# First attention of a two-layer block: score matmuls on 64 of the 128 contraction rows, two at a time

## The chip, the cores and the metric

One core of one Trainium2 chip runs the whole program. The metric is device microseconds of one execution, from the first instruction to the end. TensorE's engine is PE in the profile, its weight loader PEld; VectorE is DVE, ScalarE is ACT, GpSimd is POOL, SyncE is SP.

## The reference, cut to what matters

Two layers follow each other on `x` (2 batches of 1,024 tokens, width 256). The first is attention of the tokens over 154 context rows, with 16 heads of width 16:

```python
q = (xq @ Wq + bq).reshape(B, Lq, nh, dh)          # nh = 16, dh = 16
kv = (xkv @ Wkv + bkv).reshape(B, Lkv, 2, nh, dh)  # Lkv = 154
scores = jnp.einsum('bqhd,bkhd->bhqk', q, k) / jnp.sqrt(jnp.float32(dh))
attn = jax.nn.softmax(scores, axis=-1)
out = jnp.einsum('bhqk,bkhd->bqhd', attn, v).reshape(B, Lq, H)
return x_q + (out @ Wp + bp)
```

The second layer (a one-head attention over the same context, a router over 3 experts and a gate) follows it and is not touched by the change. Only the `scores` line above is.

## The kernel before, in words

The first attention works on 16 groups g (`GR`): 4 chunks c of 512 tokens times 4 sets gi of four heads. The 128 partitions of a group hold its four heads with 32 rows each: 16 rows of q rounded to fp32r beside the keys, and 16 rows with the same q beside the low part of the keys. So one head's scores need only 32 of the 128 rows, and the keys `ka` and `kb` are laid out block-diagonally: the columns of head k are zero on all rows but its own 32.

A group passes through these steps on PE, and the name of each is a function in the text below:

- `proj`: q of the group, six matmuls of 128x512 into bank 0 or 1; ACT rounds it to `qh` (L648).
- `rows(g, q)`, q = 0..3: token-major scores of 128 tokens, two matmuls of 308 columns (L1203), one for heads 0 and 1 into one bank of `pair`, one for heads 2 and 3 into the other. They serve only for the maxima: DVE reduces both banks at once (L894). There is one `pair`, so the next `rows` waits for the reduce (`mx_d`).
- `shift`: four small matmuls (L1211) subtract the maxima from q in its bank, and DVE makes `ql`, the low part with the shift (L903).
- `keys(g, k)`: key-major scores of head k's first 128 keys, two matmuls of 512 columns (`ka` with `qh`, `kb` with `ql`, both recorded under the helper's L1110) into bank 2 or 3. The fifth, k = 4, holds the 26 last keys of all four heads. ACT takes the exponential from the bank (L657), and a `keys` waits for the exponential that frees its bank.
- `av`: values times exponentials. Four heads write 32 partitions each, side by side (L1242), then the tails with a full 128x128 matmul (L1245).
- `uz`, `ztr`, `wproj` of the chunk before: transposes (L1255), division on DVE (L910, L913), transposes (L1266), a copy on ACT (L672), the output projection (`wp`, `zt`).

While group g makes its exponentials, group n = g + 1 makes its maxima: the generator `l0_steps` writes the order out by hand, and every engine walks through the same list. `fill[0]` to `fill[5]` are places in it for other work. Of the 16 groups, six (gi 0 and 1 of chunks 1 to 3) have `uz`, `ztr`, `wproj` in `fill[0]`, `fill[1]`, `fill[2]`. Six (gi 0, 1 and 3 of chunk 0, gi 3 of the others) have preparation matmuls for the second layer in `fill[0]` and `fill[2]`, and nothing for PE in `fill[1]`. In the four groups with gi = 2, `fill[0]` and `fill[1]` normalise and transpose the next chunk; in the last chunk they hold front work of the second layer.

Of the kernel before, what the change touches and what calls it, by code (L numbers as in the profile page):

```python
# [31 lines left out]
ACT = mybir.ActivationFunctionType  # L32
AXX = mybir.AxisListType.X

P = 128
B, LQ, D = 2, 1024, 256
LK = 154
NH, DH = 16, 16
# [3 lines left out]
CPB = NC // B  # L42
TJ = CT // P
GH = 4
NG = NH // GH
# [34 lines left out]
def build(nc, dram, out):  # L80
    ctx = ExitStack()
    with ctx:
# [10 lines left out]
        B_S, B_P, B_ST, B_U, B_TOK = [pair[:, i, :] for i in range(2)], bank[0:2], bank[2:4], bank[4], bank[5]  # L93
# [62 lines left out]
        ka, kb = keys_[:, :, :, 0:KAW], keys_[:, :, :, KAW:KAW + KBW]  # L156
# [24 lines left out]
        qh = sb("qh", (P, 2, CT), F32R, l0)  # L181
        ql = sb("ql", (P, 2, CT), F32R, l0)
        z = sb("z", (P, 2, D), F32, l0)
        zt = sb("zt", (P, 2, KC, P), F32, l0)
        pt = sb("pt", (P, GH + 1, CT), F32, l0)
# [55 lines left out]
        k_mm, kh_r, kg_r, v_mm, v_r, ka_r, kb_r = sem("k_mm"), sem("kh_ready"), sem("kg_ready"), sem("v_mm"), sem("v_ready"), sem("ka_ready"), sem("kb_ready")  # L241
# [5 lines left out]
        st_d, ex_d, av_d, u_r = sem("keyscores_done"), sem("exp_done"), sem("av_done"), sem("u_ready")  # L247
# [27 lines left out]
        def l0_steps():  # L275
            yield from (("proj", 0, 0), ("proj", 0, 1))
            for q in range(TJ):
                yield ("rows", 0, q)
                yield ("val", q)
            yield ("shift", 0)  # L280
            yield from (("proj", 1, 0), ("proj", 1, 1))
            yield ("place", 1)
            prep = 0
            for g in range(GR):
                c, gi = divmod(g, NG)
                n, m = g + 1, g + 2


                fill = [()] * 6
                first = list(front1(0))  # L290
                if c > 0 and gi < 2:
                    fill = [(s,) for t in (0, 1) for s in tile_steps(TJ * (c - 1) + 2 * gi + t)]
                if c + 1 < NC:
                    if gi == 0:
                        fill[3] += (("stats", c + 1, 0),)
                        fill[5] += (("stats", c + 1, 1),)
                    elif gi == 1:
                        fill[3] += (("rsqrt", c + 1),)
                        fill[5] += (("norm", c + 1, 0),)
                    elif gi == 2:  # L300
                        fill[0] += (("xt", c + 1, 0), ("norm", c + 1, 1))
                        fill[1] += (("xt", c + 1, 1), ("split", c + 1, 0))
                        fill[2] += (("split", c + 1, 1),)
                for at, place, i in ((GR - 4, 3, 0), (GR - 2, 0, 1), (GR - 2, 5, 2), (GR - 1, 0, 3), (GR - 1, 2, 4),
                                     (GR - 1, 3, 5), (GR - 1, 5, 6)):
                    if g == at:
                        fill[place] += tuple(first[i])

                for i in () if c and gi < 2 else (2, 5) if gi == 2 else (0, 2, 5):
                    if i == (5 if gi == 2 else 2) and c >= CPB:  # L310
                        fill[i] += (("m", 2 * (c - CPB) + gi - 2), ("m_taken", 2 * (c - CPB) + gi - 2))
                    elif prep < len(PREP):
                        fill[i] += (("prep", prep),)
                        prep += 1
                more = n < GR
                order = [("keys", g, 0), more and ("rows", n, 0), ("keys", g, 1), fill[0], ("keys", g, 2),
                         more and ("rows", n, 1), ("keys", g, 3), fill[1], ("keys", g, 4), more and ("rows", n, 2), fill[2]]
                if gi != 2:
                    order += [m < GR and ("proj", m, 0), more and ("rows", n, 3), fill[3], ("av", g), fill[4],
                              more and ("shift", n), m < GR and ("proj", m, 1)]  # L320
                else:

                    order += [more and ("rows", n, 3), fill[3], ("av", g), fill[4], more and ("shift", n),
                              m < GR and ("proj", m, 0), m < GR and ("proj", m, 1)]
                order += [fill[5]]
                for step in order:
                    if step and isinstance(step[0], str):
                        yield step
                    elif step:
                        yield from step  # L330
            assert prep == len(PREP)
# [107 lines left out]
        def walk(steps, parts):  # L439

            for s in steps:
                if s[0] in parts:
                    parts[s[0]](*s[1:])
# [146 lines left out]
        def _(act):  # L590
# [6 lines left out]
            A = nc.scalar.activation  # L597
# [49 lines left out]
                    act.wait_ge(st_d, (GH + 1) * (g - 1))  # L647
                A(qh[:, g % 2, :], B_P[g % 2][:, :], ACT.Identity, bias=sm("bq", g % NG)).then_inc(qh_r, 1)  # L648

            def keys(g, k):  # L650
                n = (GH + 1) * g + k
                act.wait_ge(st_d, n + 1)
                if k == 0 and g:
                    act.wait_ge(av_d, g)
                if n == 0:
                    act.wait_ge(v_r, 2 * B)
                A(pt[:, k, :], B_ST[n % 2][:, :], ACT.Exp, scale=DH ** -0.5).then_inc(ex_d, 1)  # L657

            def av(g):
                c = g // NG  # L660
# [73 lines left out]
                A(th[:, n % TJ, :], gz[:, n % 2, :], ACT.Tanh, scale=0.5).then_inc(th_r, 1)  # L734

            first = {"m_taken": mpiece, "nxf": nxf_, "exp": exp, "wsplit": wsplit, "router": router}
            walk(l0_steps(), {"xt": xt, "proj": proj, "keys": keys, "av": av, "zt": ztr, **first})
            walk(between_steps(), {"zt": ztr, **first})
            walk(l1_steps(), {"nxf": nxf_, "exp": exp, "wsplit": wsplit, "router": router, "hidden": hidden, "gate": gate})

# [359 lines left out]
        def _(pe):  # L1100
            mm = nc.tensor.matmul
# [5 lines left out]
            def passes(dst, terms, first=True, last=True, free=False):  # L1107

                for i, (a, b_) in enumerate(terms):
                    ins = mm(dst, a, b_, start=first and i == 0, stop=last and i == len(terms) - 1,  # L1110
                             skip_group_check=free)
                return ins
# [81 lines left out]
            def rows(g, q):  # L1194
                c, gi = divmod(g, NG)
                n = TJ * g + q
                pe.wait_ge(qh_r, g + 1)
                if gi == 0 and q == 0 and c % CPB == 0:
                    pe.wait_ge(ka_r, c // CPB + 1)
                if n:  # L1200
                    pe.wait_ge(mx_d, n)
                for s in range(2):
                    ins = mm(B_S[s][:, 0:2 * LK], qh[:, g % 2, P * q:P * q + P],  # L1203
                             ka[:, c // CPB, gi, 2 * LK * s:2 * LK * (s + 1)], start=True, stop=True)
                ins.then_inc(s1_d, 1)

            def shift(g):
# [4 lines left out]
                             skip_group_check=True)  # L1212
                ins.then_inc(nm_d, 1)

            def keys(g, k):
                c, gi = divmod(g, NG)
                b = c // CPB
                n = (GH + 1) * g + k
                if k == 0:
                    pe.wait_ge(ql_r, g + 1)  # L1220
                if n == 0:
                    pe.wait_ge(kb_r, 2 * GH)
                    pe.wait_ge(v_r, 2 * B)
                if n >= 2:
                    pe.wait_ge(ex_d, n - 1)
                if k < GH:
                    a, b_ = ka[:, b, gi, LK * k:LK * k + P], kb[:, b, gi, P * k:P * k + P]
                else:
                    a, b_ = ka[:, b, gi, LK * GH:LK * GH + P], kb[:, b, gi, P * GH:P * GH + P]
                passes(B_ST[n % 2][:, :], [(a, qh[:, g % 2, :]), (b_, ql[:, g % 2, :])]).then_inc(st_d, 1)  # L1230

            def av(g):
                c, gi = divmod(g, NG)
                b = c // CPB
                if g == 0:
                    pe.wait_ge(v_r, 2 * B)
                    pe.wait_ge(ones_r, 1)
                else:
                    pe.wait_ge(u_r, g)
                for j in range(GH):  # L1240
                    pe.wait_ge(ex_d, (GH + 1) * g + j + 1)
                    mm(B_U[32 * j:32 * j + 32, :], vmain[:, b, GH * gi + j, :], pt[:, j, :], start=True, stop=False,  # L1242
                       skip_group_check=True)
                pe.wait_ge(ex_d, (GH + 1) * (g + 1))
                mm(B_U[:, :], vtail[:, b, gi, :], pt[:, GH, :], start=False, stop=True,  # L1245
                   skip_group_check=True).then_inc(av_d, 1)
# [154 lines left out]
            def part(c, m):  # L1401
# [7 lines left out]
                for j in range(TJ):  # L1409
                    if r == 0 and q and j % 2 == 0:  # L1410
# [5 lines left out]

            rows_parts = {"uz": uz, "zt": ztr, "wp": wproj, "m": mpiece}
            front_parts = {"nxt": nxt, "score": score, "wtr": wtr}
            walk(l0_steps(), {"xt": xt, "val": val, "proj": proj, "rows": rows, "shift": shift, "keys": keys, "av": av, "prep": prep,
                              **rows_parts, **front_parts})  # L1420
            walk(between_steps(), {**rows_parts, **front_parts})
            walk(l1_steps(), {"nxt": nxt, "score": score, "wtr": wtr, "hidden": hidden, "gate": gate, "part": part})
# [58 lines left out]
```

## Time and profile before

| what | value |
|---|---|
| time, median of 3 runs | 501.45 us (498.39 to 504.14) |
| profiled execution, its span from the first to the last instruction | 497.4 us |
| PE busy | 456.4 us, 92% |
| PEld busy | 357.0 us, 72% |
| DVE, ACT, POOL busy | 326.9, 183.0, 152.1 us |
| granted TensorE clock, mean | 0.986 |
| matmuls of `keys` (L1110, `qh,keys` and `ql,keys`) | 80 and 80 |
| matmuls of `rows` (L1203) | 128 |

The profiled execution has no total time of its own in the record, only its span; the runs' times also hold what lies around the span, and their median is 4.1 us above it.

A busy share of PE counts overlapped matmuls by their modelled ends, so it says that PE was not idle, not that it ran at its peak. What a matmul costs its successor is the distance between two starts: the record of a 128x512 fp32r matmul is 0.40 us long, but the next one starts 0.23 to 0.24 us behind it. In a merged row of the timeline (xN) the length is that of all but the last one's distances plus the last record.

### The profile page before, as it was taken

The page shows a single profiled execution, that of the slowest core. Times are in us where ns is not written, and L with a number is a line of the kernel's source. Part 1 is how long each engine was busy: PE and PEld are TensorE (multiplying, and loading weights), DVE is VectorE, ACT ScalarE, POOL GpSimd, SP SyncE. Part 2 cuts the span into 40 slices and gives each one's busy share as a digit, 9 for nine tenths or more (in the row PEclk, how much of TensorE's full clock was granted, in tenths as well). Part 3 has the DMA queues.
Part 4 walks back from the last instruction along what each step waited for, and adds up shares of the span by engine and source line. Part 5 has one row for each costly group of instructions (what it writes and reads, how often), then busy time and mean ns, then how long its engine had stood idle before and what let it go on. Part 6 is the DMA issues. An engine that isn't in the chain of part 4 may idle for free.

```text
span 497.4 us, 6873 instructions
## 1 busy us (share of the span) xinstructions
PE 456.4 (92%) x2418; PEld 357.0 (72%) x2418; DVE 326.9 (66%) x794; ACT 183.0 (37%) x323; POOL 152.1 (31%) x211
## 2 busy tenths in 40 slices
PE   2657999999999999999977999999999999999994
PEld 2545665776676666766456888888888898888883
DVE  6878757376746754755877448875697657842445
ACT  1260434343344534335442254423444334532210
POOL 9347037204400400100005323354233533315333
PEclk9997999999999999999999899999999999999998
DMA  8701001610020011000011000001000010001001
GB/s 293 310 1 33 10 1 43 234 43 1 21 65 1 1 42 44 0 1 1 1 38 32 0 2 0 2 1 43 1 0 1 3 42 1 1 2 42 1 1 42
DMA packets 7314, 17.45 MB, mean 35 GB/s; under 512 B 880, under 2 KB 2288, under 8 KB 7152
## 3 DMA queue, kind: packets, MB, share of 16 engines
q1 hardware_dynamic: 5040, 11.57, 6.5%
q10 hardware_dynamic: 1584, 3.15, 1.7%
q0 software_dynamic: 656, 2.29, 1.7%
q8 instruction: 20, 0.33, 0.3%
q14 instruction: 14, 0.11, 0.1%
HBM read 14.45 MB, written 2.10 MB: 33 GB/s over the span
## 4 chain that ended last, share of the span: by engine, by line
PE 81%; DVE 11%; issue 3%; POOL 2%; ACT 2%; DMA 1%; POOLq 0%; DVEq 0%
PE bank L1110 52%; PE pair L1110 14%; PE pair L1203 4%; PE bank L1245 3%; PE bank L1242 3%; DVE lnt L783 2%; DVE nm L894 1%; PE bank L1211 1%; PE bank L1255 1%; DVE rs L767 1%; DVE keys L855 1%; DMA ctx_sb<-in_ctx 1%; DVE st L757 1%; PE bank L1266 1%; POOL rs L542 1%
## 5 line engine op out<-in xcount | busy, mean ns | idle before, releaser
L579 POOL TENSOR_TENSOR hs<-hid,hs 128x512 fp32r<-128x512 f32 x48 | 64.2, 1338 | 125.9 <-DVE hs L1063 125.9
L1110 PE MATMUL bank<-nx,w1h 128*128 128x512 f32 x224 | 74.0, 412 | 0.0
L1110 PE MATMUL pair<-w2h,hs 128*128 128x256 f32 x384 | 70.5, 282 | 0.0
L728 ACT ACTIVATE hid<-bank,ab 128x512 f32<-128x512 f32 x48 | 33.0, 689 | 89.6 <-PE bank L1110 89.5
L1110 PEld LDWEIGHTS pair<-w2h,hs 128*128 128x128 f32 x384 | 62.7, 190 | 4.4 <-POOL hs L579 0.2
L894 DVE TENSOR_REDUCE nm<-pair 128x4 fp32r<-128x616 f32 x64 | 51.1, 798 | 19.7 <-PE pair L1203 19.1
L1063 DVE CAST hs<-hid 128x512 fp32r<-128x512 f32 x48 | 20.6, 430 | 57.9 <-ACT hid L728 57.1
L657 ACT ACTIVATE pt<-bank 128x512 f32<-128x512 f32 x80 | 47.2, 598 | 28.6 <-PE bank L1110 26.0
L1110 PE MATMUL pair<-w2l,hs 128*128 128x256 f32 x192 | 54.2, 282 | 0.0
L1110 PE MATMUL bank<-wh,m_ev 128*128 128x512 f32 x112 | 44.5, 398 | 0.0
L1110 PE MATMUL bank<-nx,w1l 128*128 128x512 f32 x112 | 44.4, 396 | 0.0
L541 POOL TENSOR_TENSOR rs<-rs 128x4 f32<-128x4 f32 x21 | 4.5, 215 | 130.2 <-DVE rs L770 129.1
L1110 PEld LDWEIGHTS bank<-nx,w1h 128*128 128x128 f32 x224 | 39.3, 189 | 6.0
L1110 PE MATMUL bank<-qh,keys 128*128 128x512 f32 x80 | 38.2, 477 | 0.2 <-ACT pt L657 0.2
L1110 PEld LDWEIGHTS pair<-w2l,hs 128*128 128x128 f32 x192 | 36.2, 189 | 0.0
L1203 PE MATMUL pair<-keys,qh 128*128 128x308 f32 x128 | 31.8, 330 | 4.0 <-DVE keys L855 3.3
L1203 PEld LDWEIGHTS pair<-keys,qh 128*128 128x128 f32 x128 | 22.4, 191 | 15.3 <-issue 11.7
L666 ACT ACTIVATE u<-bank 128x512 f32<-128x512 f32 x16 | 9.6, 597 | 60.2 <-PE bank L1245 60.2
L1110 PE MATMUL bank<-ql,keys 128*128 128x512 f32 x80 | 31.6, 395 | 0.0
L1080 DVE SCALAR_TENSOR_TENSOR acc<-pair,pr,acc 128x256 f32<-128x256 f32 x48 | 20.1, 476 | 7.6 <-PE pair L1110 7.6
L1110 PEld LDWEIGHTS bank<-wh,m_ev 128*128 128x128 f32 x112 | 21.3, 190 | 5.1
L1110 PEld LDWEIGHTS bank<-nx,w1l 128*128 128x128 f32 x112 | 21.2, 189 | 5.0
(190 smaller groups left out, 921.2 us busy)
## 6 DMA issues: line engine op xcount, KB each, us to landing
stage<-in_w1n POOLq DMA_DIRECT2D x7, 256.0 KB, 3.2
w1e_sb<-in_w1e SPq DMA_DIRECT2D x1, 1792.0 KB, 7.9
x_sb<-in_x SPq DMA_DIRECT2D x3, 512.0 KB, 14.5
stage<-in_w1a SPq DMA_DIRECT2D x3, 512.0 KB, 6.7
stage<-in_ew2T SPq DMA_DIRECT2D x3, 512.0 KB, 3.9
out_x<-x_sb SPq DMA_DIRECT2D x3, 512.0 KB, 2.7
wss_sb<-in_wss SPq DMA_DIRECT2D x2, 512.0 KB, 8.7
x_sb<-in_x ACTq DMA_DIRECT2D x1, 512.0 KB, 4.9
```

The source lines that it names most:

```text
L579: g_.tensor_tensor(hs[:, q % 3, 1, :], hid[:, q % 2, :], hs[:, q % 3, 0, :], ALU.subtract).then_inc(hl_r, 1)
L657: A(pt[:, k, :], B_ST[n % 2][:, :], ACT.Exp, scale=DH ** -0.5).then_inc(ex_d, 1)
L666: A(u[:, g % NU, :], B_U[:, :], ACT.Copy).then_inc(u_r, 1)
L728: A(dst, B_H[n % 2][:, :], ACT.Silu, bias=ab1[:, m, c // CPB:c // CPB + 1]).then_inc(h_r, 1)
L783: return V.tensor_scalar(dst, src, mv[0:rows, t, 0:1], rs[0:rows, 0, t:t + 1], ALU.subtract, ALU.mult)
L894: V.tensor_reduce(nm[:, g % 2, q, :].rearrange("p (h w) -> p h w", w=32)[:, :, DH:DH + 1], pair[:, :, 0:2 * LK].rearrange("p s (a n) -> p ...
L1063: V.tensor_copy(hs[:, q % 3, 0, :], hid[:, q % 2, :]).then_inc(hh_r, 1)
L1080: V.scalar_tensor_tensor(acc[:, j, :], y_tile(j), pr[:, c % 2, j, e:e + 1], acc[:, j, :], ALU.mult, ALU.add).then_inc(y_r, 1)
L1110: ins = mm(dst, a, b_, start=first and i == 0, stop=last and i == len(terms) - 1, skip_group_check=free)
L1203: ins = mm(B_S[s][:, 0:2 * LK], qh[:, g % 2, P * q:P * q + P], ka[:, c // CPB, gi, 2 * LK * s:2 * LK * (s + 1)], start=True, stop=True)
L1242: mm(B_U[32 * j:32 * j + 32, :], vmain[:, b, GH * gi + j, :], pt[:, j, :], start=True, stop=False, skip_group_check=True)
L1245: mm(B_U[:, :], vtail[:, b, gi, :], pt[:, GH, :], start=False, stop=True, skip_group_check=True).then_inc(av_d, 1)
```

## The change

`rows` splits its two matmuls by rows: heads 0 and 1 contract over partitions 0 to 63, heads 2 and 3 over 64 to 127, which leaves out products with zeros only. `keys(g, p)` now takes a pair of heads, p and p + 2, for p = 0, 1: four matmuls of 64 rows, into bank 2 and bank 3, first both `qh` products, then both `ql` products. The tails become a step of their own, `tails(g)`, with all 128 rows, always in bank 2. A pair waits until both banks are free. The list is written anew around it.

```diff
-                order = [("keys", g, 0), more and ("rows", n, 0), ("keys", g, 1), fill[0], ("keys", g, 2),
-                         more and ("rows", n, 1), ("keys", g, 3), fill[1], ("keys", g, 4), more and ("rows", n, 2), fill[2]]
+                order = [("keys", g, 0), more and ("rows", n, 0), fill[0], more and ("rows", n, 1), ("keys", g, 1), fill[1],
+                         more and ("rows", n, 2), ("tails", g), fill[2]]
...
-            def keys(g, k):
-                n = (GH + 1) * g + k
-                act.wait_ge(st_d, n + 1)
...
-                A(pt[:, k, :], B_ST[n % 2][:, :], ACT.Exp, scale=DH ** -0.5).then_inc(ex_d, 1)
+            def keys(g, p):
+                for i in range(2):
+                    n = (GH + 1) * g + 2 * p + i
+                    act.wait_ge(st_d, n + 1)
...
+                    A(pt[:, p + 2 * i, :], B_ST[i][:, :], ACT.Exp, scale=DH ** -0.5).then_inc(ex_d, 1)
+
+            def tails(g):
+                act.wait_ge(st_d, (GH + 1) * (g + 1))
+                A(pt[:, GH, :], B_ST[0][:, :], ACT.Exp, scale=DH ** -0.5).then_inc(ex_d, 1)
...
                 for s in range(2):
-                    ins = mm(B_S[s][:, 0:2 * LK], qh[:, g % 2, P * q:P * q + P],
-                             ka[:, c // CPB, gi, 2 * LK * s:2 * LK * (s + 1)], start=True, stop=True)
+                    r = slice(64 * s, 64 * s + 64)
+                    ins = mm(B_S[s][:, 0:2 * LK], qh[r, g % 2, P * q:P * q + P],
+                             ka[r, c // CPB, gi, 2 * LK * s:2 * LK * (s + 1)], start=True, stop=True)
...
-                if n >= 2:
-                    pe.wait_ge(ex_d, n - 1)
...
-                passes(B_ST[n % 2][:, :], [(a, qh[:, g % 2, :]), (b_, ql[:, g % 2, :])]).then_inc(st_d, 1)
...
+                    pe.wait_ge(ex_d, n)
+                for i in range(2):
+                    r = slice(64 * i, 64 * i + 64)
+                    k = p + 2 * i
+                    mm(B_ST[i][:, :], ka[r, b, gi, LK * k:LK * k + P], qh[r, g % 2, :], start=True, stop=False)
+                for i in range(2):
+                    r = slice(64 * i, 64 * i + 64)
+                    k = p + 2 * i
+                    mm(B_ST[i][:, :], kb[r, b, gi, P * k:P * k + P], ql[r, g % 2, :], start=False, stop=True).then_inc(st_d, 1)
+
+            def tails(g):
...
+                pe.wait_ge(ex_d, (GH + 1) * g + 3)
+                passes(B_ST[0][:, :], [(ka[:, b, gi, LK * GH:LK * GH + P], qh[:, g % 2, :]),
+                                       (kb[:, b, gi, P * GH:P * GH + P], ql[:, g % 2, :])]).then_inc(st_d, 1)
```

`av` takes the heads in the order 0, 2, 1, 3, in which their exponentials now come. DVE's, POOL's and SP's code is the same, and no DMA is moved.

PE's order before, from the start of a group with `uz`, `ztr`, `wproj` up to `wproj` (`keys,qh` into `pair` is `rows`; bank 2 and 3 are `keys`; `ident_sb,u` is `uz`, `ident_sb,z` is `ztr`):

```order
L1110 MATMUL bank3<-qh,keys 128x512
L1110 MATMUL bank3<-ql,keys 128x512
L1203 MATMUL pair<-keys,qh 128x308 x2
L1110 MATMUL bank2<-qh,keys 128x512
L1110 MATMUL bank2<-ql,keys 128x512
L1255 MATMUL bank5<-ident_sb,u 128x128 x4
L1110 MATMUL bank3<-qh,keys 128x512
L1110 MATMUL bank3<-ql,keys 128x512
L1203 MATMUL pair<-keys,qh 128x308 x2
L1110 MATMUL bank2<-qh,keys 128x512
L1110 MATMUL bank2<-ql,keys 128x512
L1266 MATMUL bank5<-ident_sb,z 128x128 x2
```

The same stretch now (L1236 and L1240 are the 64-row matmuls of `keys`, L1209 those of `rows`, L1272 `uz`, L1283 `ztr`):

```order
L1236 MATMUL bank2<-qh,keys 128x512
L1236 MATMUL bank3<-qh,keys 128x512
L1240 MATMUL bank2<-ql,keys 128x512
L1240 MATMUL bank3<-ql,keys 128x512
L1209 MATMUL pair<-keys,qh 128x308 x2
L1272 MATMUL bank5<-ident_sb,u 128x128 x4
L1209 MATMUL pair<-keys,qh 128x308 x2
L1236 MATMUL bank2<-qh,keys 128x512
L1236 MATMUL bank3<-qh,keys 128x512
L1240 MATMUL bank2<-ql,keys 128x512
L1240 MATMUL bank3<-ql,keys 128x512
L1283 MATMUL bank5<-ident_sb,z 128x128 x2
```

Between the first and the second `rows` there were two `keys` and the transposes; only the transposes are left. The third `rows` now follows the second pair and `ztr`, and the tails stand behind it.

In a group with preparation matmuls (`ctxT_sb,pw` here), PE's order from the first `rows` to the tails was:

```order
L1203 MATMUL pair<-keys,qh 128x308 x2
L1110 MATMUL bank2<-qh,keys 128x512
L1110 MATMUL bank2<-ql,keys 128x512
L1110 MATMUL bank5<-ctxT_sb,pw 128x320 x2
L1110 MATMUL bank3<-qh,keys 128x512
L1110 MATMUL bank3<-ql,keys 128x512
L1203 MATMUL pair<-keys,qh 128x308 x2
```

and is now:

```order
L1209 MATMUL pair<-keys,qh 128x308 x2
L1115 MATMUL bank5<-ctxT_sb,pw 128x320 x2
L1209 MATMUL pair<-keys,qh 128x308 x2
L1236 MATMUL bank2<-qh,keys 128x512
L1236 MATMUL bank3<-qh,keys 128x512
L1240 MATMUL bank2<-ql,keys 128x512
L1240 MATMUL bank3<-ql,keys 128x512
L1209 MATMUL pair<-keys,qh 128x308 x2
L1115 MATMUL bank2<-qh,keys 128x512
```

The third `rows` stands directly behind the second pair, with nothing between. Over the whole program, PE's order now has 59 stretches of 64-row matmuls; 50 of them are followed by a 128-row matmul, 9 directly by the 32-column matmuls of `av`.

## Rows read from the trace of the kernel before

**Rows 1.** The page: PE's busy time (us, share, count) and its granted clock in 40 slices.

```profile
PE 456.4 (92%) x2418; PEld 357.0 (72%) x2418; DVE 326.9 (66%) x794; ACT 183.0 (37%) x323; POOL 152.1 (31%) x211
...
PEclk9997999999999999999999899999999999999998
```

**Rows 2.** Busy times by stretch, from the first `keys` to the last `av`.

```profile
49.20:235.80 186.60, 180.72 (x933) 125.37 (x933) 118.09 (x235) 78.34 (x144) 34.70 (x77) 1.00 0.11 34
```

**Rows 3.** The page's groups: busy us, mean ns of one; idle time before, releaser.

```profile
L894 DVE TENSOR_REDUCE nm<-pair 128x4 fp32r<-128x616 f32 x64 | 51.1, 798 | 19.7 <-PE pair L1203 19.1
...
L657 ACT ACTIVATE pt<-bank 128x512 f32<-128x512 f32 x80 | 47.2, 598 | 28.6 <-PE bank L1110 26.0
...
L1110 PE MATMUL bank<-qh,keys 128*128 128x512 f32 x80 | 38.2, 477 | 0.2 <-ACT pt L657 0.2
...
L1203 PE MATMUL pair<-keys,qh 128*128 128x308 f32 x128 | 31.8, 330 | 4.0 <-DVE keys L855 3.3
```

**Rows 4.** Timeline of PE, one undisturbed group with `uz`, `ztr`, `wproj`: start, length.

```profile
205.37 0.50 PE L1110 MATMUL bank<-qh,keys 128*128 128x512 f32 x1
...
205.94 0.45 PE L1203 MATMUL pair<-keys,qh 128*128 128x308 f32 x2
206.22 0.39 PE L1110 MATMUL bank<-qh,keys 128*128 128x512 f32 x1
206.46 0.39 PE L1110 MATMUL bank<-ql,keys 128*128 128x512 f32 x1
206.69 0.60 PE L1255 MATMUL bank<-ident_sb,u 128*128 128x128 f32 x4
...
209.45 1.13 PE L1110 MATMUL bank<-wp_sb,zt 128*128 128x256 f32 x4
210.23 0.58 PE L1110 MATMUL bank<-xh,wqh 128*128 128x512 f32 x1
...
211.40 0.60 PE L1255 MATMUL bank<-ident_sb,u 128*128 128x128 f32 x4
211.93 1.06 PE L1242 MATMUL bank<-pt,vmain 128*32 128x512 f32 x8
212.92 1.12 PE L1245 MATMUL bank<-pt,vtail 128*128 128x512 f32 x2
213.89 0.38 PE L1266 MATMUL bank<-ident_sb,z 128*128 128x128 f32 x2
```

**Rows 5.** Timeline of the same group, DVE, then ACT.

```profile
206.42 0.80 DVE L894 TENSOR_REDUCE nm<-pair 128x4 fp32r<-128x616 f32 x1 [0.43 <-PE pair L1203]
207.32 0.26 DVE L910 RECIPROCAL rz<-bank 128x16 f32<-128x16 f32 x1
207.61 0.42 DVE L913 TENSOR_TENSOR z<-bank,rz 128x256 f32<-128x256 f32 x1
```

```profile
209.02 0.38 ACT L672 ACTIVATE zt<-bank 128x256 f32<-128x256 f32 x1
```

**Rows 6.** Timelines of PEld near 242 us (64-column tiles) and 18 us (64-row tiles).

```profile
242.65 0.19 PEld L1110 LDWEIGHTS bank<-w1e_sb,vt 128*64 128x64 f32 x2 [0.33 <-issue]
...
18.08 0.29 PEld L1129 LDWEIGHTS pair<-ident_sb,ctx_sb 64*128 64x128 f32 x2 [0.33 <-issue]
...
18.49 0.50 PEld L1110 LDWEIGHTS bank<-csilu,wss_sb 128*128 128x128 f32 x2
```

**Rows 7.** Timeline, all engines: a reduce, and the `rows` that waits for it.

```profile
160.14 0.30 PE L1203 MATMUL pair<-keys,qh 128*128 128x308 f32 x1
...
160.48 0.80 DVE L894 TENSOR_REDUCE nm<-pair 128x4 fp32r<-128x616 f32 x1
...
161.43 0.38 PE L1203 MATMUL pair<-keys,qh 128*128 128x308 f32 x1
```

**Rows 8.** Timeline of a group with preparation: PE, then DVE.

```profile
61.87 1.24 PE L1110 MATMUL bank<-ctxT_sb,pw 128*128 128x320 f32 x4
```

```profile
63.15 0.49 DVE L940 COPY vf<-bank 128x320 f32<-128x320 f32 x1 [0.74 <-PE bank L1110]
63.67 0.22 DVE L941 COPY vt<-bank 128x64 f32<-128x64 f32 x1
```

More of the change, by code:

```diff
@@ L648, in proj @@
                 A(qh[:, g % 2, :], B_P[g % 2][:, :], ACT.Identity, bias=sm("bq", g % NG)).then_inc(qh_r, 1)
-            def keys(g, k):
-                n = (GH + 1) * g + k
-                act.wait_ge(st_d, n + 1)
[L653 to L656, printed above, removed]
-                A(pt[:, k, :], B_ST[n % 2][:, :], ACT.Exp, scale=DH ** -0.5).then_inc(ex_d, 1)
+            def keys(g, p):
+                for i in range(2):
+                    n = (GH + 1) * g + 2 * p + i
+                    act.wait_ge(st_d, n + 1)
+                    if p == 0 and i == 0 and g:
+                        act.wait_ge(av_d, g)
+                    if n == 0:
+                        act.wait_ge(v_r, 2 * B)
+                    A(pt[:, p + 2 * i, :], B_ST[i][:, :], ACT.Exp, scale=DH ** -0.5).then_inc(ex_d, 1)
+            def tails(g):
+                act.wait_ge(st_d, (GH + 1) * (g + 1))
+                A(pt[:, GH, :], B_ST[0][:, :], ACT.Exp, scale=DH ** -0.5).then_inc(ex_d, 1)
             def av(g):
@@ L736, in _ @@
             first = {"m_taken": mpiece, "nxf": nxf_, "exp": exp, "wsplit": wsplit, "router": router}
-            walk(l0_steps(), {"xt": xt, "proj": proj, "keys": keys, "av": av, "zt": ztr, **first})
+            walk(l0_steps(), {"xt": xt, "proj": proj, "keys": keys, "tails": tails, "av": av, "zt": ztr, **first})
             walk(between_steps(), {"zt": ztr, **first})
@@ L1213, in shift, with keys @@
                 ins.then_inc(nm_d, 1)
-            def keys(g, k):
+            def keys(g, p):
                 c, gi = divmod(g, NG)
                 b = c // CPB
-                n = (GH + 1) * g + k
-                if k == 0:
+                n = (GH + 1) * g + 2 * p
+                if p == 0:
                     pe.wait_ge(ql_r, g + 1)
@@ L1223, in keys @@
                     pe.wait_ge(v_r, 2 * B)
-                if n >= 2:
-                    pe.wait_ge(ex_d, n - 1)
-                if k < GH:
-                    a, b_ = ka[:, b, gi, LK * k:LK * k + P], kb[:, b, gi, P * k:P * k + P]
-                else:
-                    a, b_ = ka[:, b, gi, LK * GH:LK * GH + P], kb[:, b, gi, P * GH:P * GH + P]
-                passes(B_ST[n % 2][:, :], [(a, qh[:, g % 2, :]), (b_, ql[:, g % 2, :])]).then_inc(st_d, 1)
+                else:
+                    pe.wait_ge(ex_d, n)
[8 more added lines that the diff above has]
+            def tails(g):
+                c, gi = divmod(g, NG)
+                b = c // CPB
+                pe.wait_ge(ex_d, (GH + 1) * g + 3)
+                passes(B_ST[0][:, :], [(ka[:, b, gi, LK * GH:LK * GH + P], qh[:, g % 2, :]),
+                                       (kb[:, b, gi, P * GH:P * GH + P], ql[:, g % 2, :])]).then_inc(st_d, 1)
             def av(g):
@@ L1239, in av @@
                     pe.wait_ge(u_r, g)
-                for j in range(GH):
-                    pe.wait_ge(ex_d, (GH + 1) * g + j + 1)
+                for n, j in enumerate((0, 2, 1, 3)):
+                    pe.wait_ge(ex_d, (GH + 1) * g + n + 1)
                     mm(B_U[32 * j:32 * j + 32, :], vmain[:, b, GH * gi + j, :], pt[:, j, :], start=True, stop=False,
@@ L1418, in _ @@
             front_parts = {"nxt": nxt, "score": score, "wtr": wtr}
-            walk(l0_steps(), {"xt": xt, "val": val, "proj": proj, "rows": rows, "shift": shift, "keys": keys, "av": av, "prep": prep,
+            walk(l0_steps(), {"xt": xt, "val": val, "proj": proj, "rows": rows, "shift": shift, "keys": keys, "tails": tails, "av": av, "prep": prep,
                               **rows_parts, **front_parts})
```

## The prediction, made before the changed kernel ran

> **What bounds the kernel now.** I read the page first: PE is busy 92% of the span, at the full granted clock in nearly every slice [rows 1]. The busy times by stretch then narrow it to the first attention: from 49.2 to 235.8 us PE is busy 180.7 of 186.6 us, clock 1.00, with DVE at 118 and ACT at 78 [rows 2]. So this stage is PE's, 16 groups of 11.7 us. The page's groups say what the edited work is: 80 + 80 matmuls of `keys`, 128 of `rows`, a reduce of 798 ns behind each of the 64 `rows`, 80 exponentials of 598 ns; PE hardly ever waits for either (0.2 us for `pt`), since enough stands between [rows 3]. The timelines give the real price of each step as the distance between starts.
>
> **What it removes.** A `keys` matmul holds PE for 0.235 us (206.22 to 206.46 to 206.69), a `rows` of two for 0.28 (205.94 to 206.22) [rows 4]. If two 64-row tiles run side by side, each of 32 pairs of heads costs 0.47 instead of 0.94 and each of 64 `rows` 0.14 instead of 0.28: 15.0 + 9.0 = 24 us of array time. Can they? No row here shows row tiles together. The nearest are `av`'s 32-column tiles: eight matmuls in 1.06 us, from 211.93 to 212.92, where one full one of the same kind takes 0.43 [rows 4]; four run at once. I take full overlap; no overlap is the other bound, and a gain beyond it is excluded, since one matmul's time stays.
>
> **What it adds: changes of tiling.** Before `av` the last of four transposes starts at 211.40 + 0.60 − 0.27 = 211.73 and needs 0.11; the tiles begin at 211.93, 0.09 late. They take 2 × 0.43 + 0.02 and end at 212.81; the full matmul starts at 212.92, 0.11 late, and its record of 1.12 for two is 0.53 + 0.59 where 0.43 + 0.59 would do: the first weights were not loaded ahead, 0.10 [rows 4]. So a change of tiling with 128 columns of weights costs about 0.09 + 0.10 = 0.2 us. For 64-row tiles the one place is the prologue: before their weights the loader sits idle 0.33 us, as it does before 64-column tiles, and again before the return [rows 6]. I take 0.2 per change. Bounds: nothing (all hidden), and 0.33 (the loader's whole idle time). The Trainium skill, TensorEngine Tiling (Array Packing), Key Properties, says that a change of tiling mode drains TensorE, and this rule speaks against the change; the late starts agree. The order has 59 stretches of 64-row work: 59 entries, and 50 exits (9 go straight into `av`, whose entry was paid before). 109 × 0.2 = 22 us, which eats nearly all of the 24.
>
> **What it moves: the waits.** A `rows` waits for the reduce of the one before. From the start of the last matmul of `rows` it is 0.34 to the reduce (160.14 to 160.48), 0.80 for it, and 0.15 to the next matmul (161.28 to 161.43): 1.29 us at least from `rows` to `rows` [rows 7]. Two exponentials take about 1.2 from 0.2 behind their scores [rows 3], and the next pair needs both; so a pair can start 1.55 behind the end of the last.
>
> Six groups with `uz` (counted from the first `rows` at 0, in us): entry and pair 0.67 before it; `rows` to 0.14; exit, `uz` 0.43, entry give 0.97, but the reduce allows 1.29. Second `rows` to 1.43, pair from 1.55 to 2.02. On DVE the reciprocal and product of `uz` stand between the reduces (207.32 to 208.03) [rows 5]: the second reduce runs 1.87 to 2.67 and the third `rows` starts at 2.82, though PE, after exit, `ztr` 0.22 and entry, could at 2.64. Exit and tails: 3.63. `wproj` waits for the copy of `zt`, which stands on ACT behind the pair's second exponential, ended at 3.44; with 0.38 [rows 5] and 0.13 to PE it starts at 3.95 and ends at 4.81. Sum 5.48, against 210.23 − 205.37 = 4.86 before [rows 4]: +0.6; in the groups that DVE's statistics already delayed less, about +0.35; mean +0.5. The fourth `rows` stands alone: 0.14 + 2 × 0.2 instead of 0.28, +0.26. Together +0.76, six times: **+4.6**.
>
> Five groups with preparation, its length f (1.07 for one; its first start at 61.87, record 1.24) [rows 8]: the second `rows` at 0.54 + f is late enough for the reduce. But the third stands right behind the pair, and DVE first clears the preparation's bank (0.49 + 0.22 at most [rows 8], from 0.34 + f + 0.2), so the second reduce ends near 1.95 + f and the third `rows` starts at 2.1 + f, where PE was ready at 1.15 + f: 0.95 us idle. With tails 2.91 + f, plus 0.67 = 3.58 + f. Before: five `keys` and three `rows` are 3.19 + f, and 0.35 of short waits, 3.54 + f. The fourth `rows` goes straight into `av`: 0.14 + 0.2, +0.06. Each +0.1: **+0.5**.
>
> The three groups that normalise a chunk follow DVE's own chain (two normalisations and a split between the reduces), which is not moved: 0. The group with empty fills in the last chunk: its second `rows` is not covered by anything but the reduce, +0.3. The last group has no `rows`: 4 changes (0.8) against 0.94 saved, −0.15. The four `rows` ahead of group 0 stand alone between other matmuls: 4 × 0.26 = 1.0 if on the path, taken as half, +0.5. ACT, POOL and SP have no work added, and the second layer only starts later.
>
> Sum: 4.6 + 0.5 + 0.3 − 0.15 + 0.5 = **+5.7 us**, on a span of 497.4, so about 503; with the 4.1 us by which the median lies above the span: 501.45 + 5.7 = 507.
>
> **The rivals.**
> 1. *Changes of tiling are free, the waits hold.* With 0 for a change, an `uz` group still has its `zt` chain at 3.95 and comes to 5.28 − 4.86 − 0.14 = +0.3 (with the delayed ones, about +0.2); a preparation group to 0.47 + 2.51 = 2.98 against 3.54, with the fourth `rows` −0.7; the others −0.15 to −1. Sum 1.2 − 3.5 − 1.5 = −3.8: 498. The weight loads of row tiles would have to run ahead across the change; the prologue's idle loader speaks against.
> 2. *Faster: PE's time decides and the new waits are half of mine.* The waits in my working are 0.94 + 0.86 (the cover lost) in an `uz` group and 0.95 in a preparation group, some 15 us; with free changes and half of them, −3.8 − 7.5 = −11: 490. It decides if `rows` follows `rows` under 1.29 us or ACT takes `zt` before the pair's exponential ends. For it: 24 us is the largest single term here; against: the reduce's 0.80 is in 64 rows alike. The Trainium skill, TensorE: Matmul & The Clock Gate, Part 3, prices tiles by the span of one matmul plus some 4 ns per tile and names no change; by this alone the sum would be this rival's.
> 3. *Slower: the tiles do not overlap*, because both run at one column per cycle into two banks, twice the writes of `av`'s tiles. Each pair then takes 0.94, each `rows` 0.28. An `uz` group comes to 6.2 + 0.4 for the fourth, +1.8; preparation groups +0.85; the others 4 together: 10.6 + 4.3 + 4 = +19: 520.
> 4. *Slower: a change costs 0.33.* Part hides in the waits: an `uz` group +0.4 beyond mine, a preparation group +0.4, together +6: 513.
>
> **How the numbers follow.** Chances: forecast 0.50, rival 1 0.17, rival 2 0.14, rival 3 0.10, rival 4 0.09. The predicted time is the forecast's, 507; its own range, with the waits and the delayed groups ±4 us, is 503 to 511. The range for 8 in 10 leaves out rivals 2's lower half and 3: 494 to 516. One per cent is 5 us and is about what a measurement can tell from none: slower, over 506.5: half of the forecast and rivals 3 and 4, 0.27 + 0.19 = 0.46. Within: the rest of the forecast and most of rival 1, 0.23 + 0.13 = 0.36. Faster: 0.14 + 0.04 = 0.18.
>
> **What the profile after would show.** Overlap: the two L1236 starts a few ns apart and L1240 0.235 behind them; rival 3 would show four starts 0.235 apart. Price of a change: the first matmul behind `rows` 0.2 later than the 0.14 alone gives; under 0.05 rival 1 holds, over 0.3 rival 4. Waits: in the waits of PE, `pair` on DVE's reduce (now L899; no wait worth a row before) should rise to several us, with gaps of about 1 us before the third `rows` of preparation groups, and `wp` on ACT's copy of `zt`. PE's busy share in the stage falls below 90%. The key part of an `uz` group takes 5.5 us. I am wrong if it takes under 4.9, or if the time comes from another stage than this.

## The result and the profile after

The changed kernel takes 510.98 us in the median of 4 runs (509.13 to 512.77), the one before 499.92 (4 runs); the ratio is 1.0215, 95% interval 1.0177 to 1.0253. The forecast was 507, slower, with 494 to 516 as the range. The profiled executions span 508.4 and 497.4 us: +11.0, of which +5.7 was foreseen. Times of executions and their spans differ by 1.8 us throughout, so of the 4.1 us that the forecast put on top of the span only 1.8 lie around it; the rest is the difference between executions of the kernel before, which also came to 499.92 here where the forecast started from 501.45.

The page of the changed kernel: busy us and shares, granted clock in 40 slices, and the groups that answer to [rows 3].

```profile
PE 459.2 (90%) x2418; PEld 342.4 (67%) x2418; DVE 326.3 (64%) x794; ACT 181.6 (36%) x323; POOL 151.1 (30%) x211
...
PEclk9996997999879999999997999999999999999998
...
L899 DVE TENSOR_REDUCE nm<-pair 128x4 fp32r<-128x616 f32 x64 | 51.1, 798 | 18.4 <-PE pair L1209 17.9
...
L1209 PE MATMUL pair<-keys,qh 64*128 64x308 f32 x128 | 26.3, 401 | 13.6 <-DVE nm L899 9.9 <-DVE keys L860 3.2
```

Two things are new against [rows 1, 3]: PE waits 9.9 us for the reduce, and the clock line has dips in its 7th, 11th and 12th slice where it had none. One sign of the forecast failed: PE's busy share in the stage did not fall below 90%, it is 179.5 of 195.7 us, 92%. Busy times by stretch, the stage first; the third number from the end is the granted clock (1.00 is 2.4 GHz, 0.50 is 1.2 GHz):

```profile
51.10:246.80 195.70, 179.47 (x934) 109.33 (x934) 116.89 (x233) 77.03 (x144) 34.64 (x77) 0.96 0.10 32
37.70:44.50 6.80, 6.80 (x17) 4.16 (x18) 4.12 (x7) 0.00 (x0) 5.90 (x12) 0.50 0.14 39
47.90:51.30 3.40, 3.22 (x9) 2.18 (x9) 3.24 (x11) 0.04 (x1) 0.02 (x1) 0.51 0.27 77
78.70:85.50 6.80, 6.41 (x18) 3.22 (x22) 6.09 (x9) 2.67 (x6) 4.55 (x6) 0.50 0.16 46
129.90:133.30 3.40, 3.40 (x12) 2.55 (x13) 3.37 (x5) 2.61 (x5) 3.32 (x5) 0.50 0.22 70
143.50:150.30 6.80, 6.65 (x25) 4.00 (x25) 1.76 (x4) 1.32 (x3) 0.00 (x0) 0.50 0.27 75
150.40:246.80 96.40, 88.62 (x462) 52.70 (x459) 56.23 (x119) 40.10 (x77) 7.95 (x28) 1.00 0.04 12
```

The stage of the first attention, 186.6 us in [rows 2], takes 195.7; it begins 1.9 us later. Three stretches inside it run at 1.2 GHz, 17 us together; in [rows 2] the whole stage has clock 1.00. The two before it, 10.2 us, stand against 6.8 us in the kernel before. One more, 6.8 us from 269.8 against 3.4 there, lies in the second layer. Behind the stage nothing changed: from the last `av` to the end it is 262.5 us before and 262.6 after, so the longer stretch at 1.2 GHz there cost nothing.

PE's timeline of the group that [rows 4] shows, at full clock in both:

```profile
215.33 0.50 PE L1236 MATMUL bank<-qh,keys 64*128 64x512 f32 x2
215.67 0.39 PE L1240 MATMUL bank<-ql,keys 64*128 64x512 f32 x2
215.90 0.30 PE L1209 MATMUL pair<-keys,qh 64*128 64x308 f32 x2
216.13 0.66 PE L1272 MATMUL bank<-ident_sb,u 128*128 128x128 f32 x4
217.20 0.41 PE L1209 MATMUL pair<-keys,qh 64*128 64x308 f32 x2 [0.41 <-DVE nm L899]
217.41 0.42 PE L1236 MATMUL bank<-qh,keys 64*128 64x512 f32 x2
217.64 0.42 PE L1240 MATMUL bank<-ql,keys 64*128 64x512 f32 x2
217.99 0.44 PE L1283 MATMUL bank<-ident_sb,z 128*128 128x128 f32 x2
218.59 0.41 PE L1209 MATMUL pair<-keys,qh 64*128 64x308 f32 x2 [0.16 <-DVE nm L899]
218.93 0.50 PE L1115 MATMUL bank<-qh,keys 128*128 128x512 f32 x1
219.27 0.39 PE L1115 MATMUL bank<-ql,keys 128*128 128x512 f32 x1
219.49 1.12 PE L1115 MATMUL bank<-wp_sb,zt 128*128 128x256 f32 x4
220.27 0.58 PE L1115 MATMUL bank<-xh,wqh 128*128 128x512 f32 x1
220.69 0.40 PE L1115 MATMUL bank<-xl,wqh 128*128 128x512 f32 x1
220.92 0.39 PE L1115 MATMUL bank<-xh,wql 128*128 128x512 f32 x1
221.25 0.41 PE L1209 MATMUL pair<-keys,qh 64*128 64x308 f32 x2
```

A row of two tiles has the length of one (0.39, 0.30): they run at once, and what follows the second pair starts 0.23 behind it. Of the 32 pairs of `qh` products, 20 start 3 to 5 ns apart and 12 start 26 to 38 ns apart. The first `rows` starts at 215.90, the second at 217.20: 1.30 us, the forecast's 1.29. The third comes 1.39 behind that.

The distance between the first tails matmuls of `av` of two groups, read off the timelines of PE (one profiled execution of each kernel), tells where the 11 us lie. "Up to group 0" counts from the start of the program. The last column is the first experiment: the same order with 128-row matmuls.

| groups | before, us | after | full rows, new order |
|---|---|---|---|
| up to group 0 (preparation) | 57.47 | +1.71 | +0.71 |
| 2, 6 (normalise), 7 (preparation) | 39.35 | +4.92 | +0.84 |
| 4, 5, 8, 9, 12, 13 (with `uz`) | 67.14 | +2.78 | +6.17 |
| 1, 3, 11 (preparation) | 37.38 | +0.63 | +0.87 |
| 10, 14, 15 | 33.50 | +0.94 | +1.96 |

More than half of the loss, 6.6 us, sits in four groups, 0, 2, 6 and 7, which are the ones that meet a stretch at 1.2 GHz; group 0 met two already in the kernel before. Groups 10 and 11, of the same two kinds as 2, 6 and 7 but at full clock, lose 0.2 and 0.45.

### The profile page after: what moved, and what is told of

The parts are those of the page before. It is cut to its first block, busy times and chain, and to the rows that moved or that the text cites. A ratio compares the mean times of both kernels' runs of the same rounds, so it can differ in the third digit from the quotient of the medians.

```text
span 508.4 us, 6873 instructions
## 1 busy us (share of the span) xinstructions
PE 459.2 (90%) x2418; PEld 342.4 (67%) x2418; DVE 326.3 (64%) x794; ACT 181.6 (36%) x323; POOL 151.1 (30%) x211
## 4 chain that ended last, share of the span: by engine, by line
PE 79%; DVE 13%; issue 3%; POOL 2%; ACT 2%; DMA 1%; POOLq 0%; DVEq 0%
PE bank L1115 50%; PE pair L1115 13%; DVE nm L899 4%; PE pair L1209 4%; PE bank L1259 3%; PE bank L1262 3%; DVE lnt L788 2%; PE bank L1236 1%; PE bank L1217 1%; DVE rs L772 1%; DVE keys L860 1%; PE bank L1272 1%; DMA ctx_sb<-in_ctx 1%; PE bank L1240 1%; DVE vtail L879 1%
## 5 line engine op out<-in xcount | busy, mean ns | idle before, releaser
L658 ACT ACTIVATE pt<-bank 128x512 f32<-128x512 f32 x64 | 34.7, 595 | 31.9 <-PE bank L1240 31.8
L1209 PE MATMUL pair<-keys,qh 64*128 64x308 f32 x128 | 26.3, 401 | 13.6 <-DVE nm L899 9.9
L1209 PEld LDWEIGHTS pair<-keys,qh 64*128 64x128 f32 x128 | 13.5, 195 | 30.8 <-issue 29.6
L908 DVE SCALAR_TENSOR_TENSOR ql<-bank,small_sb,qh 128x512 fp32r<-128x512 f32 x16 | 12.0, 750 | 18.7 <-PE bank L1217 16.1
L788 DVE TENSOR_SCALAR lnt<-x_sb,mv,rs 128x256 f32<-128x256 f32 x30 | 21.4, 752 | 2.1 <-POOL rs L544 2.0
```

The source lines that it names most:

```text
L658: A(pt[:, p + 2 * i, :], B_ST[i][:, :], ACT.Exp, scale=DH ** -0.5).then_inc(ex_d, 1)
L788: return V.tensor_scalar(dst, src, mv[0:rows, t, 0:1], rs[0:rows, 0, t:t + 1], ALU.subtract, ALU.mult)
L908: V.scalar_tensor_tensor(ql[:, g % 2, :], B_P[g % 2][:, :], sm("bq", g % NG), qh[:, g % 2, :], ALU.add, ALU.subtract).then_inc(ql_r, 1)
L1209: ins = mm(B_S[s][:, 0:2 * LK], qh[r, g % 2, P * q:P * q + P], ka[r, c // CPB, gi, 2 * LK * s:2 * LK * (s + 1)], start=True, stop=True)
```

## The experiments

All ratios are to the kernel before on the same chip, 501.1 to 501.3 us there, with its clock at 0.976 to 0.988; brackets hold 95% intervals. Positions in time and distances between groups are those of one profiled execution each. The diffs are cut to the lines that matter.

**1. The new order without 64-row matmuls.** In `rows` and `keys`, all row slices become the full one:

```diff
-                    r = slice(64 * s, 64 * s + 64)
+                    r = slice(0, P)
```

> The changed kernel's order, pairs and waits, but every matmul contracts over all 128 rows, so nothing overlaps and the only changes of tiling left are av's. Theory (price of a change 0.2 us): against the change this loses 24 us of overlap and saves 109 x 0.2 = 22 us, and part of the lost overlap falls into waits for the reduce that were idle: 506 to 512, near the change's 511. Rival (changes are nearly free, the waits made the kernel slow): 511 plus most of 24, over 525. On the clock: the change's trace has 34 us at 0.5 against 10 before. If idle gaps of the new order cause it, the windows at half clock near groups 2, 6 and 7 stay and the mean clock is 0.96 to 0.97; if the 64-row matmuls cause it, they go, the mean is over 0.98 and the time is 5 us lower, 501 to 507.

Measured: 510.0 us, 1.0191 (1.0158 to 1.0224), clock 0.980 in three of four runs. The time is in the theory's range, 506 to 512; the 5 us less that were to come with the clock did not come. The half clock is gone in groups 6 and 7, and one stretch is left inside the stage, in group 2, where the kernel before has none (columns as in the table of stretches above):

```profile
77.60:81.00 3.40, 3.40 (x12) 2.48 (x11) 3.37 (x5) 2.33 (x5) 3.08 (x5) 0.50 0.13 52
```

So the 64-row matmuls lower the clock in the same order (0.960 to 0.967 against 0.972 to 0.980), and the new order takes a smaller part, since the kernel before had 0.979 to 0.986 beside these runs. Groups 0, 2, 6 and 7 lose 1.55 together where the tiled kernel loses 6.6. The new order with serial matmuls costs 1.0 us in a `uz` group, and the tiles win back 0.56 of it. The equal times are thus a balance: in the twelve groups at full clock the tiles win 4.65 us over serial matmuls, and in the other four they lose 5.1.

**2. The old order with `rows` alone on 64 rows.**

> The kernel before, in its old order, with only the 64 rows-steps split into two 64-row matmuls; each stands alone between other work. Theory: each gains 0.14 by overlap and pays an entry and an exit of 0.2 each, +0.26; 64 of them give +16.6, some hidden where PE waited: 512 to 517. Rival (a change costs nothing): 64 x -0.14 = -9, 491. Rival (0.33 per change): 64 x 0.52 = +33, 533. Half clock: with the old cover between the steps, the idle theory expects the old clock, 0.98 or more; the 64-row theory a lower one.

Measured: 511.0 us, 1.0198 (1.0177 to 1.0218), clock 0.965 to 0.973. Its timeline around one `rows`:

```profile
206.28 0.40 PE L1110 MATMUL bank<-ql,keys 128*128 128x512 f32 x1
206.61 0.41 PE L1204 MATMUL pair<-keys,qh 64*128 64x308 f32 x2
206.94 0.51 PE L1110 MATMUL bank<-qh,keys 128*128 128x512 f32 x1
207.28 0.40 PE L1110 MATMUL bank<-ql,keys 128*128 128x512 f32 x1
207.52 0.60 PE L1256 MATMUL bank<-ident_sb,u 128*128 128x128 f32 x4
```

From `ql` to the second `ql` it is 0.33 + 0.33 + 0.34 = 1.00 where [rows 4] has 0.235 + 0.28 + 0.24: +0.25 per step, my +0.26, so a change costs 0.19 to 0.20. The time, 511, lies under the range of 512 to 517: the four steps of a `uz` group give not 1.0 but +0.61 to +0.73 in groups 4, 12 and 13, and +0.28 and +0.31 in groups 5 and 9, whose part up to the next `xh,wqh` already took 5.46 us before instead of some 4.9. And this kernel has the old cover and still loses its clock (17.1 us at 1.2 GHz from 37.3, 10.2 from 143.1). Before the second of these stretches PE had not been idle at all:

```profile
138.10:143.10 5.00, 5.00 (x35) 4.27 (x34) 1.25 (x4) 1.88 (x3) 0.00 (x0) 1.00 0.15 44
143.10:153.30 10.20, 10.20 (x32) 5.27 (x32) 2.65 (x5) 1.79 (x3) 0.00 (x0) 0.50 0.19 57
```

So no idle gap took the clock there. The edit, 64-row matmuls with their changes of tiling, is all that differs from the kernel before, whose whole stage is at 1.00.

**3. and 4. Lone `rows` back to 128 rows, then a preparation step moved.**

```diff
-                    r = slice(64 * s, 64 * s + 64)
+                    r = slice(64 * s, 64 * s + 64) if g and q < 2 else slice(0, P)
```

> The changed kernel, but the third and fourth rows of every group and the four ahead of group 0 go back to 128 rows; the first two, which stand beside a pair of heads, stay tiled. Theory: each lone step saves 0.26: 12 in the groups with uz (3.1), some 1.3 in the others, 1.0 ahead of group 0: 511 - 5 = 506. In the preparation groups the third only moves inside a wait. Rival (the waits hide the changes): 509 to 511.

Measured: 508.8, 1.0155 (1.0138 to 1.0173), clock 0.960 to 0.963. A `uz` group gains 0.21 to 0.22 and not 0.52 (the five at full clock in both): the fourth step gives its share, while the third comes 1.39 behind the second in both kernels, held by the reduce. The other experiment adds

```diff
-                for i in () if c and gi < 2 else (2, 5) if gi == 2 else (0, 2, 5):
-                    if i == (5 if gi == 2 else 2) and c >= CPB:
+                for i in () if c and gi < 2 else (2, 5) if gi == 2 else (0, 1, 5):
+                    if i == (5 if gi == 2 else 1) and c >= CPB:
```

> As the kernel with the lone steps at 128 rows, and in the groups with preparation matmuls the second of them moves from behind the tails to between the second pair and the third rows-step, where PE sat idle for about 0.7 to 1 us waiting for the reduce. Theory: 5 groups x 0.7 to 0.95 less: 4 us below its neighbour, 501 to 503. Rival (what holds these groups is DVE or ACT further on): same as its neighbour within 1 us.

Measured: 509.5, 1.016 (1.0131 to 1.019): no gain, the rival's case. In the profiled executions group 1 gains 0.6 us and groups 7 and 11 lose 0.1 and 0.2; group 3, which loses 1.2, met a stretch at 1.2 GHz. The gap moved in group 11: the third `rows` is covered, and the fourth, which had the moved matmuls ahead of it, now waits.

```profile
196.82 0.40 PE L1115 MATMUL bank<-xh,wql 128*128 128x512 f32 x1
197.98 0.52 PE L1209 MATMUL pair<-keys,qh 128*128 128x308 f32 x2 [0.77 <-DVE nm L899]
```

**5. and 6. A shorter reduce, in both orders.** The maxima are taken over 32 of each head's 154 columns; the reduce falls from 798 to 290 ns.

```diff
-                                pair[:, :, 0:2 * LK].rearrange("p s (a n) -> p s a n", a=2), AXX, ALU.max).then_inc(mx_d, 1)
+                                pair[:, :, 0:2 * LK].rearrange("p s (a n) -> p s a n", a=2)[:, :, :, 0:32], AXX, ALU.max).then_inc(mx_d, 1)
```

> The changed kernel, with the maxima taken over 32 of each head's 154 columns (the rest is left out), so that the reduce falls from 0.80 us to about 0.3. Theory (the new order waits for the reduce): the waits of PE for it go (9.9 us in its trace, some of it shared with other waits): 511 - 7 = 504, between 502 and 506. Rival (price of the tile changes and clock alone): 509 to 511.

> The kernel before with the same shortened reduce. Theory: its reduces are covered by keys (waits for them are a few tenths of a us), so it gains 0 to 3 us: 498 to 501. Rival (every group waits on DVE in both orders): it gains as much as the changed one, 494.

Measured: the changed kernel 505.0 (1.0073, 1.0051 to 1.0095), the one before 495.5 (0.9887, 0.9848 to 0.9926). 505.0 is in my range and 495.5 is below it. Both gain 6 us, so my theory falls in this point: the waits for the reduce, 9.9 us in the changed kernel and 0.5 in the one before, are not what the new order pays above the old one. In the old order the gain lies in the groups whose reduces come late behind DVE's statistics (groups 2, 5, 6, 7 and 9, −0.5 to −0.7 each). In the new one a second wait stands right behind the first; a `uz` group of the changed kernel with the short reduce:

```profile
207.68 0.30 PE L1209 MATMUL pair<-keys,qh 64*128 64x308 f32 x2
207.91 0.66 PE L1272 MATMUL bank<-ident_sb,u 128*128 128x128 f32 x4
208.50 0.41 PE L1209 MATMUL pair<-keys,qh 64*128 64x308 f32 x2
209.02 0.50 PE L1236 MATMUL bank<-qh,keys 64*128 64x512 f32 x2
```

The second `rows` comes 0.82 behind the first instead of 1.30, but the pair that stood 0.21 behind it now starts 0.52 behind it: it needs both exponentials, and ACT's two run from 207.88 to 208.97. From `rows` to the pair it is 1.34 against 1.51.

**7. and 8. One tiled stretch per group, and its control.** Pair 0 with the first `rows` is tiled; heads 1 and 3 are single 128-row steps again (`one`) and give back the cover, and the other `rows` go back to 128 rows. The control has this order with 128 rows everywhere.

```diff
-                order = [("keys", g, 0), more and ("rows", n, 0), fill[0], more and ("rows", n, 1), ("keys", g, 1), fill[1],
-                         more and ("rows", n, 2), ("tails", g), fill[2]]
+                order = [("keys", g, 0), more and ("rows", n, 0), fill[0], ("one", g, 0), more and ("rows", n, 1), ("one", g, 1), fill[1],
+                         ("tails", g), more and ("rows", n, 2), fill[2]]
```

> A version that might beat both: per group one tiled stretch alone, the pair of heads 0 and 2 with the first rows-step behind it; heads 1 and 3, the tails and the other rows-steps keep 128 rows and stand between the rows-steps as cover. Theory without the clock: 0.47 + 0.14 saved against 2 x 0.2 per group, waits as before: 15 x -0.2 = -3, 498. With the clock (64-row matmuls bring windows at half speed; a quarter of the tiled work is left but near the same places): 2 to 6 us back, 499 to 504.

> The same order and waits as the version with one tiled stretch, but all matmuls on 128 rows. Theory: the order is nearly that of before, with one wait more (the pair needs both banks): 500 to 502, mean clock as before, 0.98 or more. Against it the tiled stretch alone can be read: -3 by my prices without the clock.

Measured: tiled 501.25 (0.9982, 0.9953 to 1.0011), control 501.74 (1.001, 0.9991 to 1.003), 10 runs each. No difference that can be told, but the tiled one's runs fall in two heaps by their granted clock: the four at 0.983 took 497.4 to 498.8 us, the five at 0.972 to 0.976 took 501.4 to 503.3, one at 0.982 took 501.2. The control's ten, at 0.982 to 0.985, took 500.1 to 503.3. In the two profiled executions the clock is 1.00 in the whole stage but its first 0.6 us, and the last `av` comes 3.35 us earlier with the tiles than in the control, 2.8 of it gained behind group 0's `av`: the 3 us of my prices. In five of the ten runs the time is back with a lower clock; that the clock took it is read from the two going together. The changed kernel with the short reduce shows the same pair of heaps: 500.3 and 501.5 us at 0.980 and 0.979, 504.2 to 506.3 at 0.962 to 0.969, so some 4.3 us for 0.014 of mean clock.

**9. Both tiles in the same row half.** Here, in `rows` and in `keys`, the products of partitions 64 to 127 are left out and those of 0 to 63 are done twice.

```diff
-                    r = slice(64 * i, 64 * i + 64)
+                    r = slice(0, 64)
```

> The changed kernel, but both tiles of every pair read partitions 0 to 63 (the upper half's products are left out and those of the lower half done twice). Theory (the overlap comes from different row halves): the two starts lie 0.235 us apart instead of a few ns, a pair costs 0.94 and a rows-step 0.28; 24 us of overlap lost, some of it inside waits: 522 to 530. Rival (short matmuls run faster by themselves): 511. Clock: if 64-row matmuls as such lower it, 0.96 or less stays although PE streams longer; if the stage's thinner PE time lowers it, it recovers to 0.98.

Measured: 530.25, 1.0607 (1.0552 to 1.0661), clock 0.942 to 0.951.

```profile
65.78 0.73 PE L1236 MATMUL bank<-qh,keys 64*128 64x512 f32 x2
66.35 0.61 PE L1240 MATMUL bank<-ql,keys 64*128 64x512 f32 x2
66.81 0.44 PE L1209 MATMUL pair<-keys,qh 64*128 64x308 f32 x2
```

Two matmuls in the same half take 0.61, with starts 0.23 apart, against 0.39 side by side: the overlap comes from the different halves. PE streams longest of all here, in a stage of the same order, and yet has the lowest clock of all kernels. Experiment 1 has the same order and serial matmuls too, with 128 rows, and a clock of 0.972 to 0.980. Ahead of one of the stretches at 1.2 GHz PE was busy without a gap again:

```profile
106.90:111.90 5.00, 5.00 (x33) 4.02 (x30) 1.03 (x3) 1.29 (x2) 0.00 (x0) 1.00 0.01 3
```

So it is not shorter streaming or idle time alone that lowers it.

**10. All `rows` on 128 rows, pairs tiled.**

> The changed kernel with all rows-steps at 128 rows and only the 32 pairs of heads tiled. Theory: 64 changes of tiling instead of 109, 45 x 0.17 to 0.2 = 8 to 9 us saved, 64 x 0.14 = 9 us of overlap lost, so the same within 2 us at the same clock: 509 to 512. If the clock depends on how much 64-row work there is, it rises from 0.963 to some 0.97 and the time is 2 to 3 us lower, 507.

Measured: 516.07, 1.0304 (1.0256 to 1.0351), clock 0.957 to 0.967, outside both forecasts. In this timeline the distance from the first `rows` to the second grew to 1.54:

```profile
219.93 0.55 PE L1209 MATMUL pair<-keys,qh 128*128 128x308 f32 x2
220.33 0.60 PE L1272 MATMUL bank<-ident_sb,u 128*128 128x128 f32 x4
221.47 0.52 PE L1209 MATMUL pair<-keys,qh 128*128 128x308 f32 x2 [0.55 <-DVE nm L899]
```

The same distance is 1.29 to 1.30 in the changed kernel and 1.43 in experiment 1, which has no exit there. So the second matmul's 0.14 and 0.11 of the exit lie on the chain through DVE, not beside it; I had counted them as PE's time alone, where they cancel. In groups 4, 12 and 13 this kernel takes 0.46 to 0.48 us more than the changed one, in 5 and 9 0.13 and 0.17.

**11. 128 rows in groups 0, 2, 6 and 7 only.** All other groups keep their 64-row slices; the four `rows` ahead of group 0 get 128 rows too.

> The changed kernel, with 128-row matmuls in groups 0, 2, 6 and 7 alone, in whose stretch the changed kernel's profile shows the half clock; order and waits are the same everywhere. Theory (64-row work in sparse stretches costs the clock, 5 to 6 us): mean clock 0.975 to 0.98, time 505 to 507. Rival (the half clock comes anyway, or moves to other groups): 510 to 512, clock 0.96 to 0.967.

Measured: 510.58, 1.0185 (1.0123 to 1.0247), clock 0.961 to 0.972. The rival: in the profiled execution groups 2, 6 and 7 get better (group 7 from +2.2 to +1.2) and group 0 does not (+1.8), and 13.6 us at 1.2 GHz, from 92.1 and from 105.7 us, fall on groups 3 and 4 (+2.9 and +3.0). The half clock came in other groups that still have 64-row matmuls; taking them out of four groups did not take its cost out.

## Why the prediction was right, and what it left out

**Overlap: right.** Two starts together, a row of two as long as one, and experiment 9 gives the counterproof. Rival 3 (no overlap) forecast 520; the kernel that has none takes 530, with a lower clock still.

**A change of tiling at 0.2 us: right.** The fourth `rows` of the group above: the matmul ahead of it holds PE 0.33 instead of 0.23, it takes 0.34 (0.28), and `uz` behind it 0.59 (0.53), +0.20 where I had +0.26, 0.17 per change; the isolated step of experiment 2 gives +0.25, 0.20 per change. The idle loader of [rows 6] was the right place to look. Rivals 1, 2 and 4 fall on this. The time alone would not have told: 511 is nearer to rival 4's 513 than to 507. The Trainium skill, TensorEngine Tiling (Array Packing), Key Properties, says that a change of tiling mode drains TensorE; the matmul ahead of the lone `rows`, which holds PE 0.1 us longer, agrees.

**The waits: place right, size of one wrong.** The reduce's chain is 1.30 (1.29); the third `rows` of preparation group 1 starts 1.24 behind its pair's second product, 1.0 us later than that product alone asks (0.95). But the key part of a `uz` group, 215.33 to 220.27, takes 4.94 and not 5.48, just above the 4.9 under which I had called myself wrong. Half of the first entry, 0.1, lies ahead of 215.33, where I counted all of it inside. The wait of `wproj` for `zt`, 0.32 in my working, did not come: ACT does two exponentials in 1.09, takes `zt` at 219.04 and is done at 219.43, before the tails leave PE. The rest is `wproj` itself, 0.78 (0.86). In the six groups the key part grows by 0.05 in the mean, where I had 0.5; what they lose is 0.2 in the mean ahead of their first pair (0.1, the entry, in groups 4 and 13, 0.2 to 0.3 in the others) and 0.2 at the fourth `rows`. So six `uz` groups cost 2.8 and not 4.6.

**The groups around: nearly.** Groups 1, 3 and 11 cost +0.6 (0.3 foreseen), 10, 14 and 15 +0.9 (0.15), 1.1 us more than foreseen together.

**What failed is a step that the sum does not have: the clock.** I read 1.00 in [rows 2] and took it for the stage's own property. The changed kernel spends (1 − 0.963) × 508.4 × 2 = 38 us at 1.2 GHz, the profiled one before (1 − 0.986) × 497.4 × 2 = 14, 3 to 4 of them in both at the very end. Groups 0, 2, 6 and 7 lose 6.6 where my steps come to 0.7 and where the same order costs 1.55 with full rows: by these two differences the clock costs 5 to 6 us. This is an estimate, since it takes what is left over for the clock's. The 4.3 us that go with 0.014 of clock, or 14 us at 1.2 GHz, in the runs of the changed kernel with the short reduce give about 0.3 us per us, and with the 20 us more that this kernel has up to the last `av`, some 6 us too. What I had in the sum, corrected: 2.8 + 0.6 + 0.9 + 0.7 = 5.0, near the forecast's 5.7, partly because its errors (−1.8 and +1.1) run against each other; the clock is a second term, as large. The wide range, 494 to 516, held; the forecast's own, 503 to 511, held by 0.02 us, and that was luck, since about half of the loss came from a term that the sum does not have.

That the 64-row form lowers the clock is shown by three pairs, each in one order: experiment 1 against the change (0.972 to 0.980 against 0.960 to 0.967), experiment 2 against the kernel before (0.965 to 0.973 against 0.979 to 0.986), and experiment 9 against experiment 1, both serial (0.942 to 0.951 against 0.972 to 0.980). The 64-row matmuls come with changes of tiling, and no run has one without the other. The number of changes alone does not order the kernels: 64 of them in experiment 10 have 0.957 to 0.967, 109 in the changed kernel 0.960 to 0.967, the same 109 in experiment 9 0.942 to 0.951. Idle time may have a part elsewhere: in the 5 us ahead of the stretch in group 2 PE was busy 2.97 us in the changed kernel and 3.40 in experiment 1, and both lost the clock there. Why the stretches begin where they do, and what of these matmuls lowers the clock, stays open.

The version with one stretch per group is the fastest of the tiled ones and is not shown to beat the kernel before.

## What to carry to other kernels

Row tiles of different halves overlap fully here, but each stretch of them pays 0.4 us for its two changes, so it must save clearly more; one pair of 512-column matmuls side by side saves 0.235. Gather them, and count the stretches in the order first. Before giving steps that cover a chain (matmul, reduce, matmul) to something faster, add up the chain: 1.29 us here was covered by exactly what the change merged. And read the granted clock of the stage as a quantity that the change can move: here a matmul form that was meant to be cheaper cost some 5 us in it, with the neighbours slowed too.

## What the runs showed that I had not expected

A kernel with 256 of its 288 score matmuls on 64 rows lost 0.02 of mean granted clock (0.963 against 0.98 to 0.986), with serial 64-row matmuls 0.03 to 0.04 (0.942 to 0.951), although PE was busy 92% of the span in the latter. Among runs of one and the same kernel, 0.014 of clock went with 4.3 us. And a second wait can stand exactly behind the first: a reduce shortened by 0.5 us brought a `uz` group's next pair 0.17 us forward.
